# Decoder kernel: two heads per transposed block in the first attention, maxima added by 16-row matmuls, stacks loaded whole, one scan of 512 columns

## The reference, cut to what matters

```
x = x + L0_attn (layernorm(x))          # 16 heads of 16, causal, ternary weights
x = x + L0_xattn(w, u, layernorm(x), ctx)   # WKV recurrence along 128 steps
x = x + L0_ffn  (layernorm(x))          # sigmoid-gated, ternary weights, hidden 704
x = x + L1_attn (layernorm(x))          # 32 heads of 8, 8 key heads, rotary
x = x + L1_xattn(layernorm(x), ctx)     # windows and alibi over two key sets
x = x + L1_ffn  (layernorm(x))          # low-rank experts, top 2 of 6
```

```
q, k, v = bitlinear(x, w_q), bitlinear(x, w_k), bitlinear(x, w_v)   # 16 heads, D = 16
attn = where(causal, q k^T / sqrt(D), NEG_INF)
out  = bitlinear(softmax(attn) v, w_o)
```

```
p, q = A2 * p + E2 * v, A2 * q + E2
y    = (A * p + E * v) / (A * q + E)
```

## Time and profile before

| | us |
|---|---|
| runs | 815.83, 820.05, 820.11 (median 820.05) |
| profiled execution | 819.26 |
| its span, first to last instruction | 817.3 |
| TensorE busy (matmul) | 661.6 (81%) |
| VectorE busy | 567.4 (69%) |
| ScalarE busy | 504.6 (62%) |
| GpSimd busy | 303.7 (37%) |

### The profile page before, as it was taken

One profiled execution on the slowest core, in us unless ns is written; L12 is line 12 of the kernel. 1 busy time (PEld: TensorE's weight loads), 2 busy tenths in 40 slices (PEclk: granted clock), 3 DMA queues, 4 the chain that ended last, 5 costly groups with the idle time before them and its releaser, 6 DMA issues. The chain is left out here.

```text
span 817.3 us, 19059 instructions
## 1 busy us (share of the span) xinstructions
PE 661.6 (81%) x6724; PEld 391.7 (48%) x6724; DVE 567.4 (69%) x1616; ACT 504.6 (62%) x1213; POOL 303.7 (37%) x493
## 2 busy tenths in 40 slices
PE   0378888856567778889999877999999999988985
PEld 0145555544345556644544344554454544544553
DVE  6467787878999996677887737555555555557786
ACT  2457778866677655478788762556565665565431
POOL 5212444474677875955655212112111121101110
PEclk9988999977587899999999999999999999999999
DMA  3798986640030000353464423322342224220001
GB/s 117 167 193 169 182 143 121 118 91 11 17 142 14 1 2 1 68 96 67 71 95 67 73 53 72 68 47 48 67 68 51 47 50 79 52 41 2 34 32 40
DMA packets 176238, 58.76 MB, mean 72 GB/s; under 512 B 164560, under 2 KB 174224, under 8 KB 175888
## 3 DMA queue, kind: packets, MB, share of 16 engines
q1 hardware_dynamic: 176144, 57.55, 36.1%
HBM read 15.25 MB, written 2.10 MB: 21 GB/s over the span
## 5 line engine op out<-in xcount | busy, mean ns | idle before, releaser
L1155 DVE TENSOR_REDUCE l1x_neg_max<-bank 128x2 f16<-128x448 f32 (+1 forms) x192 | 117.7, 636 | 99.7 <-PE bank L1273 99.5
L1210 ACT ACTIVATE l1x_probs<-bank 128x512 f32<-128x512 f32 x192 | 106.2, 596 | 46.0 <-PE bank L1294 29.7
L881 DVE TENSOR_REDUCE l1a_neg_max<-bank 128x4 f16<-128x512 f32 x128 | 83.3, 684 | 29.1 <-PE bank L970 28.1
L930 ACT ACTIVATE l1a_probs<-bank 128x512 f32<-128x512 f32 x128 | 69.5, 595 | 30.6 <-PE bank L984 29.8
L1108 POOL TENSOR_TENSOR l1x_rstd<-l1x_var_eps,minus_half 128x1 f32<-128x1 f32 x16 | 8.8, 548 | 206.7 <-DVE l1x_var_eps L1139 206.7
L1648 PE MATMUL bank<-mix_xT_parts,w_ternary 128*128 128x256 f16 x384 | 58.3, 313 | 8.6 <-DVE mix_hidden L1542 8.6
L1648 PEld LDWEIGHTS bank<-mix_xT_parts,w_ternary 128*128 128x128 f16 x384 | 41.2, 112 | 23.2 <-DVE mix_hidden L1542 10.1
L648 ACT ACTIVATE l_probs<-bank 128x512 f32<-128x512 f32 x64 | 36.8, 594 | 22.1 <-PE bank L715 21.5
L575 DVE TENSOR_REDUCE l_neg_max<-bank 128x4 f16<-128x512 f32 x64 | 41.0, 676 | 8.5 <-PE bank L701 8.2
L698 PE MATMUL bank<-causal_masks,ident_bf 128*128 128x512 bf16 x64 | 28.2, 441 | 22.3 <-DMA l_kT<-k_stack 21.6
L1471 POOL TENSOR_TENSOR mix_hidden_parts<-mix_hidden,mix_hidden_parts 128x256 f16<-128x256 f32 x48 | 35.6, 748 | 21.2 <-ACT mix_hidden_parts L1600 21.2
(11 more groups left out here) (271 smaller groups left out, 1907.8 us busy)
## 6 DMA issues: line engine op xcount, KB each, us to landing
x_residual<-x_in SPq DMA_DIRECT2D x4, 512.0 KB, 4.9
mix_ctx_in<-ctx_in SPq DMA_DIRECT2D x16, 128.0 KB, 2.1
l1x_ctx_in<-ctx_in SPq DMA_DIRECT2D x16, 128.0 KB, 2.1
out_dram<-moe_out SPq DMA_DIRECT2D x16, 128.0 KB, 1.7
w_f<-w_in SPq DMA_DIRECT2D x2, 704.0 KB, 6.2
w_attn_f<-w_l_in SPq DMA_DIRECT2D x1, 1024.0 KB, 6.1
q_stack<-q_begin_in SPq DMA_DIRECT2D x1, 1024.0 KB, 5.1
l1x_qT<-l1x_neg_maxT SPq DMA_DIRECT2D x64, 2.0 KB
```

The costliest lines, as they stand in the source:

```text
L881: dve.tensor_reduce(mm[:, 16 * j + 4 * s:16 * j + 4 * s + 4], b_s[c % 3][:].rearrange("p (r k) -> p r k", k=P), AX.X, ALU.max, negate=True ...
L930: act.activation(prob[:, c, :], b_st[c % 2][:], ACT.Exp).then_inc(s_exp, 1)
L1155: dve.tensor_reduce(mm[:, first:first + count], scores, AX.X, ALU.max, negate=True).then_inc(s_max, 1)
L1210: act.activation(prob[:, c, :], b_st[c % 2][:], ACT.Exp).then_inc(s_exp, 1)
```

## The change

In l0 two heads share a 128-column block: each has 64 columns. The stacks of l0 become tiles of its own, half as large, and each transposing DMA moves 1024 columns. Scores of a pair of heads are two matmuls over 64 rows each, the one on rows 0 to 63, the other on 64 to 127, into two banks. S and ST come as two pieces a row instead of four, each filling both banks. The maxima are no longer copied into `qT` by DMA: 16 matmuls a row, with a column of the identity repeated as weights and the 16-row `neg_maxT` as the moving operand, add them to the transposed scores. The column of ones in the keys, the DMA and its semaphore go. The stacks for l1a and l1x are loaded whole as four more entries of `late_loads`; `refit_stacks` goes. GpSimd clears only l0's value tile and the small tiles. In mix, p and q stand side by side and one scan of 512 columns runs over both; ScalarE writes the decay twice for it (the decay at the first step of a sequence is zero there, so the scan starts anew at column 256). The orders of l0 are new, those of the other stages are the same pieces with new planned times.

```diff
-        G+3 M+2"""),
+        G+1"""),
     ("l0", "pool"): order("""
-        F1c-1 F8c.0-2 F8c.1-2"""),
+        F8c.1+2 F1c+4 F8c.0+3"""),
     ("l0", "dve"): order("""
-        S.2 S.3 T1b-3 T3-3 F1b+3 T3b-3 F1c+3 T3c-3 F8b.0+2 F8b.1+2 T3s-3 F3b+3 F3c+3 F3d+3 T5-3 S.0+1 S.1+1 F8s+3
-        F1+4 T1-2"""),
+        S.2 F1+4 T3b-3 S.3 F1b+4 T3c-3 F3b+3 F8b.0+2 F3c+3 T3s-3 F3d+3 F1c+4 F8b.1+2 F8s+3 T5-3 S.0+1 S.1+1 T1-2
+        T1b-2 T3-2"""),
     ("l0", "act"): order("""
-        T3e-3 F3+3 T4-3 F8v+2 ST.0 F3e+3 F3f+3 ST.1 ST.2 F5+3 OE-1 ST.3 F8a.0+3 M+1 F8a.1+3 T3d-2"""),
+        F5+2 OE-2 ST.2-1 ST.3-1 F3+3 F8a.0+2 F8a.1+2 T3d-3 M T3e-3 F3e+3 T4-3 ST.0 F3f+3 F8v+2 ST.1"""),
     ("l0", "pe"): order("""
-        S.0+1 T4-3 ST.0 T5-3 S.1+1 ST.1 ST.2 T1-2 S.2+1 F5+3 S.3+1 ST.3 F7+3 M+1 PV"""),
+        T4-3 S.0+1 T5-3 F5+3 T1-2 ST.1 S.1+1 F7+3 PV M+1 ST.0+1"""),
...
-    cleared = [net.q_stack, net.k_stack, net.v_stack, net.v_l1a, net.hw] + net.mm
+    cleared = [l0_vs, net.hw] + net.mm
...
-SETUP, SPREAD, LOADS = (0.0, 0.22, 4.0, 0.5, 5.1), (6.0, 7.3, 0.66, 2.0), (1.4, 0.7, 4.4, 0.6)
-PACE = {"l0": (0, 8, 9.85, 9.38), "mix": (156.5, 2.25, 15.97, 10.62), "l1a": (286.0, 1.74, 8.18, 14.66), "l1x": (456.5, 6.0, 15.02, 26.37), "moe": (712.0, 5.96, 4.55, 4)}
+SETUP, SPREAD, LOADS = (0.05, 0.22, 3.95, 0.1, 5.1), (6.2, 7.3, 0.66, 2.0), (1.3, 0.7, 4.4, 0.55, 14.2, 0.2)
+PACE = {"l0": (0, 8, 8.0, 11.73), "mix": (141.0, 2.25, 15.97, 7.96), "l1a": (270.0, 2.17, 8.18, 14.66), "l1x": (437.5, 5.91, 15.02, 26.37), "moe": (695.0, 5.96, 4.55, 4)}
...
-            if piece == "M":
-                sp.wait_ge(s_mt, b + 1)
-                sp.dma_start(qt[MROW:MROW + 1, b % 3, :, :], mt[:]).then_inc(s_md, 16)
...
-                wait(pe, s_max, b * NC_ + c - 1)
-                ps = b_s[c % 2]
-                pe.matmul(ps[:], net.identb[:], net.cmask[:, 0, :], start=True, stop=False, skip_group_check=True)
+                wait(pe, s_max, b * NC_ + 2 * c)
+                for j in range(2):
+                    pe.matmul(b_s[j][:], net.identb[:], net.cmask[:, 0, :], start=True, stop=False, skip_group_check=True)
                 for x in range(4):
...
+                    for j in range(2):
+                        rows = slice(64 * j, 64 * j + 64)
+                        ins = pe.matmul(b_s[j][:, P * x:P * x + P], qt[rows, b % 3, 4 * c + x, :], kt[rows, b % 3, 4 * c + x, :],
+                                        start=False, stop=x == 3, skip_group_check=True)
...
             elif piece == "ST":
+                wait(pe, s_exp, b * NC_ + 2 * c)
...
+                        pe.matmul(b_st[j][:, P * x:P * x + P], kt[rows, b % 3, 4 * c + x, :], qt[rows, b % 3, 4 * c + x, :],
+                                  start=False, stop=False, skip_group_check=True)
                 if c == 0:
-                    pe.wait_ge(s_md, 16 * (b + 1))
...
+                    pe.wait_ge(s_mt, b + 1)
+                for j in range(2):
+                    for x in range(4):
+                        h = 8 * c + 4 * j + x
+                        ins = pe.matmul(b_st[j][:, P * x:P * x + P], net.ident16[0:NH, h:h + 1].to_broadcast([NH, P]), mt[:],
+                                        start=False, stop=x == 3, skip_group_check=True)
                 ins.then_inc(s_st, 1)
...
-                for x in range(2):
-                    ins = dve.tensor_tensor_scan(st[:, c, x, 1:2 * P + 1], ex[:, c, 0], ex[:, c, 1 + x], 0.0,
-                                                 ALU.mult, ALU.add)
-                ins.then_inc(s_scan, 1)
+                dve.tensor_tensor_scan(st[:, c, 1:4 * P + 1], ex[:, c, 0:2].rearrange("p x t -> p (x t)"),
+                                       ex[:, c, 2:4].rearrange("p x t -> p (x t)"), 0.0, ALU.mult, ALU.add).then_inc(s_scan, 1)
...
+                          (net.q_stack[:], dram["q_begin"]), (net.k_stack[:], dram["k_begin"]), (net.v_stack[:], dram["v_begin"]),
+                          (net.v_l1a[:].rearrange("p c g e -> p (c g e)"), dram["v_begin"][:, 0:768]),
```

More of the change, by code:

```diff
@@ new lines @@
+    ("mix", "act"): (1.483, 1.502, 1.637, 1.673, 1.692, 1.709, 1.718, 1.823, 1.843, 1.859, 1.951, 2.005, 2.024, 2.058,
+        2.086, 2.108, 2.264, 2.298, 2.404, 2.42, 2.451),
+    ("mix", "pe"): (0.184, 0.228, 0.33, 0.442, 0.47, 0.483, 0.632, 0.73, 0.822, 0.903, 1.023, 1.113),
+    ("l1a", "sp"): (0.042, 0.477),
+    ("l1a", "pool"): (2.596, 2.877, 2.992, 3.064, 3.178),
+    ("l1a", "dve"): (1.709, 1.717, 1.79, 1.863, 1.884, 1.925, 1.949, 2.022, 2.096, 2.116, 2.189, 2.214, 2.287, 2.326,
+        2.522, 2.595, 2.668),
@@ new lines @@
+    ("l1a", "act"): (2.726, 2.915, 2.974, 3.032, 3.064, 3.128, 3.152, 3.211, 3.269, 3.355, 3.374, 3.406, 3.465, 3.523,
+        3.568, 3.668),
+    ("l1a", "pe"): (2.737, 2.813, 2.848, 2.877, 2.977, 3.044, 3.08, 3.108, 3.266, 3.309, 3.324, 3.368, 3.452, 3.496,
+        3.602, 3.63, 3.667),
+    ("l1x", "sp"): (1.475, 1.522, 1.929),
+    ("l1x", "pool"): (0.36, 0.398),
+    ("l1x", "dve"): (1.341, 1.346, 1.421, 1.461, 1.571, 1.607, 1.618, 1.639, 1.662, 1.761, 1.796, 1.906, 1.917, 1.952,
+        1.957, 1.971, 2.006, 2.15, 2.185, 2.221, 2.302),
@@ new lines @@
+    ("l1x", "act"): (1.686, 1.736, 1.746, 1.778, 1.82, 1.852, 1.884, 2.096, 2.128, 2.16, 2.192, 2.223, 2.259, 2.291,
+        2.322, 2.333, 2.358, 2.39, 2.421, 2.52, 2.552),
+    ("l1x", "pe"): (1.665, 1.718, 1.77, 1.799, 1.832, 1.857, 1.886, 2.06, 2.075, 2.107, 2.136, 2.206, 2.238, 2.249,
+        2.282, 2.336, 2.369, 2.467, 2.5, 2.529, 2.633),
+    ("moe", "sp"): (0.705,),
+    ("moe", "pool"): (1.166,),
+    ("moe", "dve"): (-0.017, 0.06, 0.114, 0.133, 0.26, 0.324, 0.4, 0.474, 0.538, 0.596, 0.669, 0.762, 0.832, 0.903,
+        0.932),
@@ L354 @@
+    ("moe", "act"): (1.431, 2.295, 2.342),
+    ("moe", "pe"): (-0.262, 0.216, 0.264, 0.422),
 }
@@ L397, in prepare_windows @@
 def prepare_windows(pool, net):
-    at = [clock("l0", NB, 12 + 0.5 * k) for k in range(9)]
+    at = [clock("l0", NB, LOADS[4] + LOADS[5] * k) for k in range(9)]
     yield at[0]
@@ L450, in sem @@
         return net.sem(f"l0_{name}")
-    X, D, NH, NC_, MROW = net.X, 16, 16, 4, 64
+    X, D, NH, NC_ = net.X, 16, 16, 4
+    stage = Net()
     banks = net.banks
@@ L480, in l0_stage @@
     s_to, s_oq, s_t4, s_ot, s_y, s_x = sem("o_magic_ready"), sem("oq_ready"), sem("oT_in_psum"), sem("oT_ready"), sem("y_ready"), sem("x_updated")
-    stage = Net()
-    q_slots = [qs[:, p2, :, 0:64].rearrange("p h (t d) -> p h t d", d=D) for p2 in range(2)]
-    k_slots = [ks[:, p2, :, 0:64].rearrange("p h (t d) -> p h t d", d=D) for p2 in range(2)]
+    q_slots = [qs[:, p2].rearrange("p x (j t d) -> p (x j) t d", j=2, d=D) for p2 in range(2)]
+    k_slots = [ks[:, p2].rearrange("p x (j t d) -> p (x j) t d", j=2, d=D) for p2 in range(2)]
     def twice(src):
@@ L750, in l0_stage @@
     stage.s_x = s_x
-    stage.s_bt, stage.s_pv = s_bt, s_pv
     return stage
@@ L1897, in build @@
         net.banks = [ctx.enter_context(nc.psum_tensor(f"bank{i}", [P, 512], F32)) for i in range(8)]
-        begin = setup_stage(nc, net, dram, Arena(nc, base + EVEN, ODD))
-        l0 = l0_stage(nc, net, dram, begin, Arena(nc, base, EVEN))
+        even = Arena(nc, base, EVEN)
+        l0_vs = even.tile("l0_v_ones", [P, 3, 16, 32])
+        begin = setup_stage(nc, net, dram, Arena(nc, base + EVEN, ODD), l0_vs)
+        l0 = l0_stage(nc, net, dram, begin, even, l0_vs)
         mix = mix_stage(nc, net, dram, l0, Arena(nc, base + EVEN, ODD))
@@ L1909, in _ @@
         def _(sp):
-            merge(*[stage.programs["sp"](sp) for stage in stages], refit_stacks(sp, net, dram, l0))
+            merge(*[stage.programs["sp"](sp) for stage in stages])
             moe.stored(sp)
```

121 lines of the change are left out of this document (41 added, 80 removed).

## The result

The changed kernel takes 807.75 us in the median of four runs (806.88, 807.47, 808.02, 809.21), beside 818.1 for four runs of the kernel before on the same chip: ratio 0.9876, 95% interval 0.9838 to 0.9914. Timed again in a later job it took 808.53 (six runs), ratio 0.9869 (0.9845 to 0.9894). It is faster by 1.2%; the forecast of 797 was too low by 10.7 us, and its range (787 to 809) just holds the time. The profiled execution took 809.21, with a span of 807.1 against 817.3.

What follows compares the result with a forecast made beforehand. Prediction: later stages full (VectorE, then TensorE); block 0 bound by ScalarE in good periods, all engines waiting in bad ones. 819.26 - 5.4 (start) - 18.2 (13 periods) + 2 (hand-over) - 1 (scans) = 796.7, say 797; range 787 to 809.

Steps and rivals of the forecast that it cites:

- Start: Before row 0 of block 0: fewer clears and narrower key transposes bring row 0 earlier, -5.4 us in all.
- The 4.35 us at L249: First scaling of attention weights on VectorE: GpSimd through with clears sooner, so 4.83 us becomes 0.48.
- 13 periods: Block 0, row 0 to row 13: every period falls from 9.20 to 7.8 us, saving 18.2 us.
- Period 7.8: One row of block 0: TensorE's 7.5 us plus 0.3 of waits; lower end 7.4, upper end 8.6.
- the cover: Block 0: TensorE work between pieces hides each 1.5 us wait for the readers of both banks.
- Only ST.0 to ST.1 is tight: Block 0, transposed scores: 1.7 us of TensorE work against ScalarE's 1.9 between its exponentials; 0.3 us added.
- Hand-over and scans: Block 0 to second block: +2 us (bounds -4 and +8); one 512-column scan instead of two of 256: -1.
- Signs: What would show it: L249 at 0.48 us, row 0 near 31, row 13 near 132, DMA under 0.6, ScalarE over 0.9.
- A: Second block: the merged order, not the engines, decides its start; last UP 17.5 us earlier, time 802; chance 0.18.
- B: Block 0: pair-wise banks stall ScalarE, period 8.6 us, time 807; chance 0.14 together with D.
- D: Block 0: key transposes do not land sooner, a row loses only the maxima's 2.0 us; time as B; chance 0.14 with B.
- C: Block 0: cover fails, two 1.5 us waits bare per row, period 10.5, time 830, deciding from 9.6; chance 0.05.

Runs made afterwards that it cites:

- e4b: Changed kernel plus eight clears of an unread spare tile at the start of GpSimd's queue; 812.22 us, ratio 0.9918 to the kernel before.
- e5: Changed kernel plus one more 1024-column transposing transfer per block of block 0, into an unread tile; 807.78 us, ratio 0.9850 to the kernel before.
- e6: Changed kernel with planned starts of l1a, l1x and moe 4 us earlier; 810.88 us, ratio 0.9892 to the kernel before.
- e2: Changed kernel with the planned step between VectorE's three sums over later weights back at 0.5 turns from 0.1; 804.89 us, ratio 0.9815 to the kernel before.
- e3: Changed kernel without the sixteen 16-row matmuls per block that add the negated maxima; 796.04 us, ratio 0.9710 to the kernel before.
- e1: Changed kernel with F5, the transpose of the normalised values, issued behind T1-2 on TensorE; 808.55 us, ratio 0.9859 to the kernel before.
- e9: Changed kernel with F3 (normalised rows) moved into ScalarE's gap ahead of ST.2's exponentials; 807.97 us, ratio 0.9899 to the kernel before.
- e14: Changed kernel with TensorE's, ScalarE's and VectorE's lists of block 0 reordered together; 810.56 us, ratio 0.9887 to the kernel before.
- e8: Changed kernel with ST.1, the second half of the transposed scores, ahead of F5 on TensorE; 828.32 us, ratio 1.0098 to the kernel before.
- e11: Changed kernel with F3 in ScalarE's gap, F7 ahead of S.1 on TensorE, S.3 behind S.2 on VectorE; 821.15 us, ratio 1.0018 to the kernel before.
- e15: The changed kernel, unaltered, timed again in a later job; 808.53 us, ratio 0.9869 to the kernel before.

## Why the prediction was too low

Span by span, forecast and measured: start -5.4 and -4.0; row 0 to row 2 15.6 and 22.0; eleven further periods 85.8 and 90.0; the rest +1 and +1.3. The four differences, 1.4, 6.4, 4.2 and 0.3, make, but for rounding, the 12.4 us between the forecast change (-22.6) and that of the span (-10.2).

- **Start, right in mechanism, too large.** The 4.35 us at L249 were forecast and e4b shows their cause. By the Trainium skill, "SBUF — State Buffer", "Who interferes with whom", the one that issues first blocks the other for its whole instruction, from which the prediction read a wait for one clear only; in e4b it waited from 11.95 to 16.34, through some three clears of 0.9 us, the one of 1.38 and the short ones behind, so here the measurement decides. The smaller transposes gave 1.8 us more, not 1: row 0's scores begin at 26.24, 5.8 us earlier. The same 1.8 were lost behind them, since row 0's maxima come 6.3 us behind its first scores (4.5 in the earlier trace rows). The second half of the scores, S.1, needs both banks and waits 0.93 us for the maxima of the first: this uncovered wait of the pair-wise banks the forecast did not price for the fill.
- **"13 periods": the failed step.** The sum took every period alike from row 0. The fill takes 22.0 us for two, more than before (19.3). Row 0 to row 1 is 1.5 us over the forecast, of which 1.2 go with the lower level of the clock (8.1 us in e5, e6 and e4b). The hole is 4.9 over. By e2, 2.1 of these are the three sums in a lump, an edit in the diff that the prediction did not cost at all, and 1.0 of the 2.1 would only move into the next period. Of the other 2.8 the trace shows the 2.3 us wait behind the first sum and the lower level after it; no run takes them away.
- **Period 7.8: the engine right, the cover wrong.** TensorE's 7.5 us were right (7.41), piece by piece. TensorE of the changed kernel, ST.1 and then S.1:
```profile
99.58 0.59 PE L694 MATMUL bank<-causal_masks,ident_bf 128*128 128x512 bf16 x2
100.11 0.40 PE L698 MATMUL bank<-l_qT,l_kT 64*128 64x128 f16 x8
100.43 0.62 PE L705 MATMUL bank<-l_neg_maxT,ident_f 16*128 16x128 f16 x8
100.98 0.60 PE L681 MATMUL bank<-causal_masks,ident_bf 128*128 128x512 bf16 x2
101.52 0.40 PE L685 MATMUL bank<-l_kT,l_qT 64*128 64x128 f16 x8
101.85 0.39 PE L669 MATMUL bank<-w_l_ternary,l_xT 128*128 128x256 f16 x2
```
  From start to start ST takes 1.40 us (by the forecast's prices 0.44 + 0.24 + 0.44 + 3 x 0.09 = 1.39) and S 0.87 (0.86). Eight heads take 0.32 to 0.33 with a change of rows behind them, where 0.24 was their price without one. What failed is "Only ST.0 to ST.1 is tight". The cover was counted for banks that wait for pairs; it was not asked what the fillers wait for. F5 needs the values' bank, which ScalarE empties behind the copy of T4, an exponential and F3f:
```profile
97.31 0.37 ACT L647 COPY l_oT<-bank 128x256 f16<-128x256 f16 x1
97.57 0.60 ACT L631 ACTIVATE l_probs<-bank 128x512 f32<-128x512 f32 x1
98.06 0.42 ACT L601 ACTIVATE l_xq<-l_x_magic 128x256 f16<-128x256 f32 x1
98.37 0.47 ACT L612 ACTIVATE l_v_ones<-bank,l_scales 128x256 f32<-128x256 f32 x1
...
101.09 1.09 ACT L631 ACTIVATE l_probs<-bank 128x512 f32<-128x512 f32 x2 [0.67 <-PE bank L705]
```
  This is ScalarE of the changed kernel. TensorE's F5 starts at 98.99, and only S.0 and T5, done at 98.35, stand beside the four. Then ScalarE idles 0.67 itself, for ST.1. e3 shows that TensorE's work is on the ring; e1, e9 and e14 show that moving pieces only moves the wait. That the period is set by several rings of the same length fits all of them, but no order that shortens it was found, so it is argued, not shown.
- **Hand-over and scans, right in sum by luck.** Forecast were +2 at the hand-over to the second block and -1 for the scans, together +1 up to that block's end, and nothing behind it. Measured are -1.6 up to its end and +2.7 in l1a. Sixteen 512-column scans keep VectorE busy 22.2 us where 32 of 256 columns took 25.5, on an engine 94.72 of 100 busy: the -1 may have been somewhat small. No run has the scan alone.
- **Signs.** Right: no key waits, L249's first row at 0.48 us, clock not lower in block 0. Wrong: row 0 at 32.5 (31), row 13 at 144.6 (132), DMA 0.65 (under 0.6), ScalarE 0.85 (over 0.9), the second block's end 13.1 us earlier (22). VectorE's 0.947 lies at the edge of its sign (0.95). The mean period of 8.62 passes the forecast's own sign of being wrong (8.3); the even ones do not.
- **Rivals.** A, at 802, is not borne out: its plan moves 17.5 us, and the second block ended 13.1 earlier, 1.6 more than row 13. B gave the right time, 807, by a wrong path. Its mean of 8.6 us is the measured 8.62 over thirteen periods, but the even ones take 8.18, the rest is the fill, and ScalarE's wait for scores fell from 22.1 to 13.3 us. D is wrong: the key transposes land after 3.3 us instead of 4.9. C did not happen in the changed kernel, but its mechanism exists: in e8 ST.1 meets its pair of exponentials uncovered, the period is 9.83 and the time 828, where C had 830 and a deciding point of 9.6; e11 at 9.57 is at par with before.

## What to carry to other kernels

Before pricing a period, list for every filler in the in-order queue what it waits for itself; a filler that hangs on the engine it should cover is no cover. Price the first rounds of a pipeline apart from the steady ones, together with every one-off job that the plan puts between them. Where the period is a ring over several in-order engines, take work out of the ring: removing 1.1 us of TensorE work gave 0.82 per block, while none of six reorderings gave anything. And before a difference of two executions is put down to an edit, compare the clock level of their first rounds: here it moved row 13 by more than most edits did.

## What the hardware did unexpectedly

- In e8 TensorE is idle for 1.03 us at one place in each block. Two blocks with that wait (65.32 and 74.28 us) ran at the upper level; later every second one fell to the lower (mean granted clock 0.87 over 108 us, against 0.99). The fall cost more than the wait: the idle time per block went from 0.64 to 1.03, the period from 8.18 to 8.9 to 9.0 in blocks at the upper level and to 11.6 in the others, 9.83 in the mean.
- A run of eight short GpSimd clears holds up one VectorE scaling as long as two clears of 3.51 us did (4.39 and 4.83 us). The scaling ends at 16.34 and 16.50 us, when GpSimd's last small clears begin (16.19 and 16.34): what counted in both is the queue without a gap, not the length of one instruction.
- Executions with the same code in block 0 differ by 2.9 us at row 13 (142.36 in e6, 145.24 in e15), nearly all of it between rows 0 and 1, where TensorE's matmuls run at the upper level from 32.2 us on in e6 and from about 42 on in e15.
